# Attention output and expert activations placed 96 instead of 64 bytes behind a 128-byte boundary of SBUF

## The chip, the core and the metric

The kernel runs on one core of a Trainium2 chip. The metric is the device time of one execution in microseconds (us). The engines are named as in the profile: PE is TensorE's matmuls, PEld its weight loads (the load of the operand that stays in the array), DVE is VectorE, ACT is ScalarE, POOL is GpSimd, SP is SyncE, which issues most transfers.

## What is computed

A gated block of a Flamingo-like model, in float32, on 32 sequences of 128 tokens of width 256:

```python
x = x + tanh(g_xattn) * xattn(layernorm(x), ctx)          # 16 heads of 64, inner width 1024
x = x + tanh(g_ffn)   * moe(layernorm(x))

# xattn: q = x @ Wq, k = ctx @ Wk, v = ctx @ Wv; softmax(q k^T / 8) v; then  out @ Wo + bo
# moe:   logits = x @ gate_w.T ; two of eight experts for each token, at most 1024 tokens an expert
#        h  = relu(de @ fc1_w.T + fc1_b)      (256 -> 1024)
#        eo = h @ fc2_w + fc2_b               (1024 -> 256)
#        out = sum over the two experts of eo * gate
```

## The kernel before, in words

The program has two stages, one after the other.

**Attention** (`attention`) goes through 8 groups of 4 sequences (512 tokens), and in each through 8 pairs of heads: 64 steps. The products are split: each operand is cut into a high part of type float32r and a low part, the rest, also float32r, and a product is three matmuls (high by high, high by low, low by high). ACT writes the high part out of PSUM (line 698), DVE subtracts and writes the low part (line 809). The output of the heads is kept that way in `aT_h` and `aT_l`, 8 x 512 columns each. Once in a group PE multiplies them with the output weights: `project_out`, lines 558 to 560, in two bursts of 48 matmuls, one into `query_bank`, one into `out_bank`. There `aT_h` or `aT_l` is the stationary operand (128 columns, so 512 bytes of each partition) and `wo_h` or `wo_l` the moving one (256 columns). The last group is done in pieces at the end (lines 654 to 656).

**Experts** (`experts`) goes through 16 halves of experts, 512 token slots each. For each half PE runs, in this order: 48 matmuls *up* of 512 columns (lines 1195 to 1197; stationary `w1_h`/`w1_l`, moving `rT_h`/`rT_l`), 8 transposes of the next half's rows (line 1179; stationary `rows`, moving `ident`), and 96 matmuls *down* of 256 columns (lines 1209 to 1211; stationary `hid_h` and `hid_l`, moving `w2_h`/`w2_l`, which for every second expert are the tiles called `w_split` in the profile). After each sixth *up* matmul ACT writes `hid` (line 1245), DVE casts it to `hid_h` (line 1304) and subtracts for `hid_l` (line 1306). Of each *down* tile DVE adds the bias into `eo_raw` (line 1315), ACT scales it (line 1253) and POOL scatters it (line 1151). The rows of an expert come from the DRAM tensor `disp` by one transfer a half, in pieces of 1032 bytes, to `rows_0` or `rows_1`; POOL's indirect transfers out of `packed` filled `disp` in the attention stage (line 407).

The order of the work is written out by hand on every engine, with semaphores between them. Tiles are allocated in the order of the calls, one behind the other, each from a multiple of 32 bytes. Three tiles that nobody reads or writes shift what lies behind them. `round_up` (1824 bytes) puts the weights at byte 20480 of each partition. `line_up` stands in front of `aT_h`, `line_up_hid` in front of `hid_h`:

```python
ROUND_UP = (20480 - 18656) // 4
LINE_UP = 64 // 4
...
    pT = sb("pT", [P, 2, TOK])
    sb("line_up", [P, LINE_UP])
    aT_h, aT_l = sb("aT_h", [P, NP, TOK], f32r), sb("aT_l", [P, NP, TOK], f32r)
    packed = sb("packed", [P, GB, W])
...
    hid = [sb(f"hid{n}", [P, TOK]) for n in range(2)]
    sb("line_up_hid", [P, LINE_UP])
    hid_h, hid_l = sb("hid_h", [P, HK, TOK], f32r), sb("hid_l", [P, HK, TOK], f32r)
    eo_raw = sb("eo_raw", [P, GB, D])
    rows = [sb("rows_0", [P, GB, W])]
```

In the built program the tiles begin at these bytes of a partition (remainder by 128):

| tiles | before | remainder |
|---|---|---|
| w1, w2, wq, wk, wv, wo parts; xT, c parts; q_sb, k_sb, v_sb, work, probs_odd, pT; rT_h, rT_l, hid | many | 0 |
| ident | 17888 | 96 |
| aT_h, aT_l, packed | 182336, 198720, 215104 | 64 |
| tri, ones, iota, bias_o, gate_sb | 219232 and on | 96 |
| logitsT | 222432 | 96 |
| hid_h, hid_l, eo_raw, rows_0, rows_1 | 122944, 139328, 155712, 159808, 164032 | 64 |
| b2_0, b2_1 | 168160, 169184 | 96 |

Of the kernel before, what the change touches and what calls it, by code (L numbers as in the profile page):

```python
# [25 lines left out]
BIG = 65536.0  # L26
V_AHEAD = 2
ROUND_UP = (20480 - 18656) // 4
LINE_UP = 64 // 4


def pass_gate(eng, sem):
# [87 lines left out]
def attention(nc, ctx, block, sem, x_v, out_v, disp, ctxT, g_x, g_f, wq, wk, wv, wo, bo, gateT, fc1T, fc2, shared):  # L120
# [4 lines left out]
    def sb(name, shape, dt=f32):  # L125
        return ctx.enter_context(nc.sbuf_tensor(name, shape, dt))
# [23 lines left out]
# [3 lines that stand above are left out]
# [895 lines left out]
def experts(nc, ctx, block, sem, out_rows, disp, fc1T, fc1b, fc2, fc2b, shared):  # L1048
# [4 lines left out]
    def sb(name, shape, dt=f32):  # L1053
        return ctx.enter_context(nc.sbuf_tensor(name, shape, dt))
# [7 lines left out]
# [3 lines that stand above are left out]
# [290 lines left out]
```

## Time and profile before

| | |
|---|---|
| runs of the kernel | 995.57 us median of 3 (991.43, 995.57, 996.29) |
| the profiled execution | 994.87 us, its span 993.1 us |
| mean granted TensorE clock | 0.983 |
| busy: PE, PEld, DVE, ACT, POOL | 949.4, 823.4, 676.3, 508.1, 281.8 us |
| instructions | 18998 |

A page of the profile gives the busy time of each engine, the span in 40 slices, the transfers, the chain of waits that ended last, and the costliest groups of instructions. Matmuls are pipelined: each is shown with 0.28 us or so, from its start until its result is out, while the next one starts after some 0.12 us. So the distance between starts, or the length of a burst over the number of its matmuls, is what a matmul costs, and not its own duration.

### The profile page before, as it was taken

The numbers are of one execution on the slowest core, as the hardware profiler recorded it, in microseconds if no ns is written. First come the engines' busy times: TensorE is split into PE (matmuls) and PEld (weight loads), VectorE is DVE, ScalarE is ACT, GpSimd is POOL, SyncE is SP. The second block draws the span as 40 slices with busy tenths as digits, with TensorE's granted clock in tenths as the row PEclk, the third lists the DMA queues.
The fourth block names the chain that finished last, engine by engine and source line by source line (L and its number), as shares of the span: only waits on it lengthen the run. The fifth ranks groups of instructions, "written<-read, shape, count | busy, mean of one in ns | idle before, by whom it ended". The sixth has DMA issues, their size and how long they took to land.

```text
span 993.1 us, 18998 instructions
## 1 busy us (share of the span) xinstructions
PE 949.4 (96%) x7199; PEld 823.4 (83%) x7199; DVE 676.3 (68%) x1542; ACT 508.1 (51%) x1573; POOL 281.8 (28%) x293
## 2 busy tenths in 40 slices
PE   7799999999999999999999888999999999999996
PEld 5587877888878878878888786999999999999995
DVE  5768687686785886886776862757575665657572
ACT  3567376465664773673754621535444343435352
POOL 6803025024033043042041133222222223232222
PEclk8989999999999999999999998999999999999998
DMA  9096003011020021021011015254342435252521
GB/s 259 22 298 194 22 2 107 23 41 67 22 86 24 22 92 38 2 86 44 1 44 44 13 52 187 66 117 101 76 128 50 128 49 130 49 130 56 141 53 22
DMA packets 63099, 76.63 MB, mean 77 GB/s; under 512 B 6033, under 2 KB 55096, under 8 KB 63008
## 3 DMA queue, kind: packets, MB, share of 16 engines
q1 hardware_dynamic: 50720, 59.18, 20.0%
q0 software_dynamic: 12288, 16.23, 9.0%
q8 instruction: 58, 0.95, 0.4%
q14 instruction: 33, 0.27, 0.1%
HBM read 46.52 MB, written 29.49 MB: 77 GB/s over the span
## 4 chain that ended last, share of the span: by engine, by line
PE 73%; ACT 11%; DVE 8%; POOL 3%; DMA 2%; issue 2%; SPq 1%; POOLq 0%; DVEq 0%; another core or an unknown queue 0%
PE down L1211 6%; PE down L1210 6%; PE down L1209 6%; PE up L1195 6%; PE up L1196 6%; PE up L1197 6%; PE score L545 4%; ACT probs_odd L733 4%; ACT work L733 4%; PE out_bank L533 4%; PE probT L520 4%; DVE negmax L913 2%; PE rT L1179 2%; PE query_bank L466 2%; PE query_bank L464 2%
## 5 line engine op out<-in xcount | busy, mean ns | idle before, releaser
L1151 POOL DMA_INDIRECT out_dram<-eo,index x64 | 99.4, 1553 | 282.2 <-ACT eo L1253 250.4
L1245 ACT ACTIVATE hid<-up,b 128x512 f32<-128x512 f32 x128 | 88.3, 690 | 84.8 <-PE up L1197 84.8
L733 ACT ACTIVATE probs_odd<-score,negmax 128x128 f32<-128x128 f32 x256 | 91.3, 382 | 44.6 <-DVE negmax L913 44.6
L733 ACT ACTIVATE work<-score,negmax 128x128 f32<-128x128 f32 x256 | 91.4, 383 | 42.8 <-DVE negmax L913 42.8
L407 POOL DMA_INDIRECT disp<-packed,slots x64 | 68.8, 1075 | 133.8 <-DVE slots L904 92.4
L913 DVE TENSOR_REDUCE negmax<-score 128x4 f32<-128x512 f32 x128 | 82.0, 682 | 28.1 <-PE score L545 27.7
L698 ACT ACTIVATE k_sb<-key_bank 128x512 f32<-128x512 f32 x64 | 38.8, 606 | 112.8 <-PE key_bank L489 111.5
L1253 ACT ACTIVATE eo<-eo_raw,gate 128x256 f32<-128x256 f32 x64 | 30.9, 506 | 122.4 <-DVE eo_raw L1315 122.4
L1306 DVE TENSOR_TENSOR hid_l<-hid,hid_h 128x512 fp32r<-128x512 f32 x128 | 88.6, 693 | 4.4
L921 DVE COPY pT<-probT 128x512 f32<-128x512 f32 x128 | 82.2, 682 | 8.7 <-PE probT L520 7.4
L1315 DVE TENSOR_TENSOR eo_raw<-down,b 128x256 f32<-128x256 f32 x64 | 25.8, 423 | 86.4 <-PE down L1211 86.4
L545 PEld LDWEIGHTS score<-k_sb,q_sb 64*128 64x128 f32 x1024 | 66.8, 189 | 18.7 <-ACT q_sb L698 16.0
L545 PE MATMUL score<-k_sb,q_sb 64*128 64x128 f32 x1024 | 70.4, 277 | 11.7 <-ACT q_sb L698 11.7
L1304 DVE CAST hid_h<-hid 128x512 fp32r<-128x512 f32 x128 | 55.2, 432 | 33.1 <-ACT hid L1245 32.7
L1209 PE MATMUL down<-w_split,hid_h 128*128 128x256 f32 x256 | 72.6, 284 | 0.0
L533 PE MATMUL out_bank<-pT,v_sb 128*64 128x128 f32 x1008 | 69.8, 281 | 2.3 <-DVE xT_l L809 1.8
L1209 PE MATMUL down<-w_h,hid_h 128*128 128x256 f32 x256 | 72.0, 281 | 0.0
L1211 PE MATMUL down<-w_split,hid_l 128*128 128x256 f32 x256 | 71.9, 281 | 0.0
L1210 PE MATMUL down<-w_split,hid_h 128*128 128x256 f32 x256 | 71.9, 281 | 0.0
L1210 PE MATMUL down<-w_l,hid_h 128*128 128x256 f32 x256 | 71.3, 279 | 0.0
L1211 PE MATMUL down<-w_h,hid_l 128*128 128x256 f32 x256 | 71.3, 279 | 0.0
L533 PEld LDWEIGHTS out_bank<-pT,v_sb 128*64 128x64 f32 x1008 | 54.5, 138 | 10.6 <-DVE xT_l L809 3.1
(253 smaller groups left out, 2788.8 us busy)
## 6 DMA issues: line engine op xcount, KB each, us to landing
rows<-disp SPq DMA_DIRECT2D x18, 516.0 KB, 5.4
w_raw<-fc1T_dram SPq DMA_DIRECT2D x9, 1024.0 KB, 8.3
w_raw<-fc_dram SPq DMA_DIRECT2D x9, 1024.0 KB, 10.9
disp<-fixed SPq DMA_DIRECT2D x1, 8256.0 KB, 33.8
rows<-x_dram SPq DMA_DIRECT2D x16, 512.0 KB, 4.3
out_dram<-rows SPq DMA_DIRECT2D x8, 512.0 KB, 3.1
c_raw<-ctxT_dram SPq DMA_DIRECT2D x8, 256.0 KB
c_raw<-ctxT_dram SPq DMA_DIRECT2D x16, 128.0 KB
```

The costliest lines, as they stand in the source:

```text
L407: pool.indirect_dma_start(out=disp[:, :], out_offset=bass.IndirectOffsetOnAxis(ap=slots[:, j, b:b + 1], axis=0), in_=packed[:, b, :], in_o ...
L533: last = mm(bank[hh * DH:(hh + 1) * DH, b * P:(b + 1) * P], v_sb[:, j // 4, b, cols], pT[:, hh, b * P:(b + 1) * P], start=True, stop=True)
L545: last = mm(score[hh][:, t], q_sb[r, t], k_sb[u % 2][r, t], start=True, stop=True)
L733: last = nc.scalar.activation(probs[w % 2][:, c, :], score[hh][:, b * P:(b + 1) * P], ACT.Exp, bias=negmax[:, w % 2, c:c + 1], accum_out=s ...
L913: V.tensor_reduce(negmax[:, w % 2, hh * GB:(hh + 1) * GB], score[hh][:, :].rearrange("p (i k) -> p i k", i=GB), axis=AX, op=ALU.max, negat ...
L921: V.tensor_copy(pT[:, hh, :], probT[hh][:, :]).then_inc(pt_done, 1)
L1151: pool.indirect_dma_start(out=out_rows[:, :], out_offset=bass.IndirectOffsetOnAxis(ap=index[half][:, i:i + 1], axis=0), in_=eo[half][:, i, ...
L1209: mm(o, hid_h[:, k, t], w2_h[par][:, k, :], start=(k == 0), stop=False)
L1210: mm(o, hid_h[:, k, t], w2_l[par][:, k, :], start=False, stop=False)
L1211: last = mm(o, hid_l[:, k, t], w2_h[par][:, k, :], start=False, stop=(k == HK - 1))
L1245: nc.scalar.activation(hid[m % 2][:, :], up[m % 2][:, :], ACT.Relu, bias=b1[par][:, m:m + 1]).then_inc(s_hid, 1)
L1306: V.tensor_tensor(hid_l[:, m, :], hid[m % 2][:, :], hid_h[:, m, :].bitcast(f32), ALU.subtract).then_inc(s_hid_split, 1)
```

## The change

```diff
@@ -26,7 +26,7 @@
 BIG = 65536.0
 V_AHEAD = 2
 ROUND_UP = (20480 - 18656) // 4
-LINE_UP = 64 // 4
+LINE_UP = 96 // 4
```

Both `line_up` and `line_up_hid` grow from 64 to 96 bytes. Everything that is allocated behind them in its stage moves up by 32 bytes: in attention `aT_h`, `aT_l` and `packed` then begin 96 bytes behind a multiple of 128, `tri`, `ones`, `iota`, `bias_o`, `gate_sb` and `logitsT` on one, and the small statistics and routing tiles 32 bytes further; in the experts `hid_h`, `hid_l`, `eo_raw`, `rows_0` and `rows_1` begin 96 bytes behind, `b2_0` and `b2_1` on a multiple. `ident` and all weights stay. No instruction is added, taken away or moved on any engine or queue; only addresses in SBUF differ.

## Rows read from the trace of the kernel before

**Rows 1.** The page: busy time with share and count, and the slices of PE
```profile
PE 949.4 (96%) x7199; PEld 823.4 (83%) x7199; DVE 676.3 (68%) x1542; ACT 508.1 (51%) x1573; POOL 281.8 (28%) x293
...
PE   7799999999999999999999888999999999999996
```
**Rows 2.** Windows of both stages: stretch, length, busy by engine, clock, DMA share, GB/s
```profile
615.20:982.80 367.60, 367.60 (x2430) 336.43 (x2429) 235.48 (x447) 163.14 (x239) 95.68 (x62) 1.00 0.40 92
100.00:550.00 450.00, 441.10 (x3776) 370.87 (x3775) 336.27 (x846) 265.82 (x1054) 117.79 (x139) 1.00 0.13 42
```
**Rows 3.** Windows of the first three bursts of up, PE alone
```profile
615.20:626.20 11.00, 10.97 (x48) 0.99 0.56 203
638.42:649.34 10.92, 10.92 (x48) 1.00 0.95 235
684.21:695.12 10.91, 10.91 (x48) 1.00 0.95 226
```
**Rows 4.** Windows of bursts of down, PE alone: four of the sixteen
```profile
627.03:638.42 11.39, 11.39 (x96) 1.00 0.02 2
650.13:661.52 11.39, 11.39 (x96) 1.00 0.18 37
673.23:684.21 10.98, 10.98 (x96) 1.00 0.00 0
695.91:707.30 11.39, 11.39 (x96) 1.00 0.21 48
```
**Rows 5.** Windows of project_out into out_bank, PE alone: two of seven
```profile
106.32:111.97 5.65, 5.65 (x48) 1.00 0.01 3
...
384.87:390.31 5.44, 5.44 (x48) 1.00 0.02 3
```
**Rows 6.** Timeline of PE: start us, duration us, line, tiles; in the third burst
```profile
674.46 0.28 PE L1210 MATMUL down<-w_l,hid_h 128*128 128x256 f32 x1
674.58 0.28 PE L1211 MATMUL down<-w_h,hid_l 128*128 128x256 f32 x1
674.69 0.28 PE L1209 MATMUL down<-w_h,hid_h 128*128 128x256 f32 x1
```
**Rows 7.** Timeline of PE: bursts at full clock that are shorter than their loads
```profile
8.12 1.17 PE L112 MATMUL key_bank<-ident 128*128 128x128 f32 x9
```
**Rows 8.** The same, later
```profile
584.22 1.95 PE L685 MATMUL out_bank<-gate_sb,work 128*128 128x8 f32 x16
```
**Rows 9.** Instructions of single lines: duration ns min/median/max, first and last start
```profile
L1211 PEld LDWEIGHTS down<-w_split,hid_l x256: 187/188/188, 627.2 to 937.2; 128*128 128x128 f32 x128
...
L1306 DVE TENSOR_TENSOR hid_l<-hid,hid_h x128: 691/693/694, 618.2 to 972.4; 128x512 fp32r<-128x512 f32 x128
```
**Rows 10.** The same for ones as stationary operand
```profile
L591 PEld LDWEIGHTS query_bank<-mask,ones x14: 192/192/192, 140.6 to 557.8; 128*128 128x128 f32 x14
```
**Rows 11.** The same for line 698 and line 809 between 110 and 560 us
```profile
L698 ACT ACTIVATE aT_h<-out_bank x52: 597/609/614, 116.2 to 555.0; 128x512 fp32r<-128x512 f32 x52
...
L698 ACT ACTIVATE logitsT<-query_bank x7: 277/278/279, 127.2 to 544.3; 128x128 f32<-128x128 f32 x7
L698 ACT ACTIVATE xT_h<-query_bank x6: 597/599/600, 148.4 to 495.6; 128x512 fp32r<-128x512 f32 x6
```
**Rows 12.** The costliest groups: busy, mean ns of one, idle before and releaser
```profile
L1304 DVE CAST hid_h<-hid 128x512 fp32r<-128x512 f32 x128 | 55.2, 432 | 33.1 <-ACT hid L1245 32.7
```
**Rows 13.** Instructions of line 1315
```profile
L1315 DVE TENSOR_TENSOR eo_raw<-down,b x64: 410/425/427, 634.4 to 983.4; 128x256 f32<-128x256 f32 x64
```
**Rows 14.** The chain of waits between the stages: start us, us, what
```profile
604.54 2.40 DMA disp<-packed,slots
607.21 3.65 DMA rows<-disp
610.91 1.97 PE rT L1179 x8
```

## The prediction

> **What bounds the kernel.** I read the page first, then the windows by stage, the windows burst by burst, and last the starts of single matmuls. The page shows PE busy for 949.4 us of the 993.1, and in nearly every slice at nine tenths or more [rows 1]. By stage it is plainer: from 615.2 to 982.8 us, the experts, PE is busy for all of 367.6 us at full clock, DVE for 235.5, ACT for 163.1; from 100 to 550 us, attention, PE for 441.1 of 450 [rows 2]. So a microsecond of PE counts in full in the experts and nearly so in attention, and time on DVE, ACT or POOL counts only once its slack is gone.
>
> PE's time there is a number of matmuls by the distance between their starts. The chip shows two speeds for one and the same work. The reader should see this in the bursts of down: 96 matmuls take 11.39 us in one, and 10.98 us in the third [rows 4]. I read all sixteen: twelve take 11.39, and the four that take 10.98 are the first halves of the odd experts. The tiles and their addresses are the same in the second half of those experts, where a burst takes 11.39. Project_out does the same thing: 48 matmuls take 5.65 us in four of the seven bursts into out_bank, and 5.44 in the last three [rows 5]; the other seven follow the burst beside them, which makes eight slow and six fast. By matmul that is 5.65/48 = 118 ns against 5.44/48 = 113 ns, and inside a fast burst each start is 0.11 or 0.12 us behind the last [rows 6]. A burst keeps the speed with which it comes out of its first matmuls. A row for up shows nothing of it: 10.91 to 11.00 us for 48 matmuls of 512 columns, 227 ns each [rows 3]; up reads no tile that moves, except that it waits for DVE and ACT.
>
> **The change, part by part.** No instruction comes, goes or changes its place, so no count changes and no queue is passed by anything. What may change is the duration of instructions that touch a tile with a new address. Those are five kinds.
>
> *Loads of aT and hid as stationary operand*: 1536 in the experts' down, 672 in project_out, 48 in the last group. They lie under a matmul: a load takes 187 to 188 ns from start to end [rows 9], but one can start every 112 ns, as two bursts show whose matmuls are too short to hide it. Nine matmuls on ident, which lies 96 bytes behind a multiple of 128, take 1.17 us; less the last one's own 0.275 us, that is 0.90/8 = 112 ns [rows 7]. Sixteen with a stationary tile on a multiple of 128 take 1.95 us: (1.95 - 0.26)/15 = 113 ns, the first distance included [rows 8]. So a load from 96 costs what a load from 0 costs, and ones, at 96 too, is loaded in 192 ns [rows 10], like ident. I take no change in the interval of a load: 112 ns, below the 113 of a fast burst. The bounds: below, all bursts fast; above, all slow. Both ends are rows of the same work. All fast: 12 x (11.39 - 10.98) = 4.9 us and 8 x (5.65 - 5.44) = 1.7, so 6.6 us less. All slow: 4 x 0.41 = 1.6 and 6 x 0.21 = 1.3, so 2.9 us more. Since the speed already differs between bursts with the same addresses, I expect another mixture and no trend: 0 is my term.
>
> *Writes and reads of aT and hid by ACT and DVE*: ACT writes aT_h, at 64, in 609 ns and xT_h, at 0, in 599; logitsT, at 96, has a quarter of the columns and takes 278 [rows 11]. 599 - 278 = 321 ns for 384 columns is 0.84 ns a column, and 278 - 128 x 0.84 = 171 ns are fixed; nothing is left that would be due to an address. DVE needs 693 ns for hid_l [rows 9] and 432 for hid_h [rows 12]. Together 1.13 us for every six matmuls of up, which take 6 x 0.227 = 1.36 us. So even a loss there has 0.24 us, 21%, of cover in each of 128 blocks; this is what hides the term. 0.
>
> *Reads of b2 and writes of eo_raw*: b2 goes from 96 to 0, eo_raw from 64 to 96. The addition takes 425 ns [rows 13] and runs beside down, 4 in a burst of 11 us. Without that cover it would still be off PE's path. 0; the last one of the program alone stands on the path, with tens of nanoseconds at most.
>
> *Small tiles*: tri, ones, gate_sb and logitsT go from 96 to 0; they are loaded or read some 20 times in a group, at intervals that rows 7 and 8 show equal for 96 and 0. 0.
>
> *Transfers into rows and out of packed*: they run under PE's work, but for one: at the seam of the stages the last scatter of 2.40 us and the first load of rows of 3.65 us stand in the chain [rows 14]. The pieces of 1032 bytes start at a multiple of 8 bytes before and after; the load's nearest row is itself. I take 0, with 0.2 us either way. A rule of the Trainium skill speaks against the change here: "DMA: Bandwidth & Descriptors", section "How a descriptor splits into AXI transactions", says that a read transaction starts from a 256-byte boundary, and what lies between it and the start is fetched in beats of 32 bytes for nothing. If that held for the SBUF side of these pieces, each would need 36 beats instead of 35, an estimate from that page of 3% on the load, or 0.1 us more in the sum; no row of this trace shows two starts for one size, so it stays out.
>
> The sum: 994.87 us of the profiled execution plus 0 = 994.9. That execution is 0.7 below the median of the three runs, 995.57, and these runs spread over 4.9 us. That spread is the size of twelve bursts of down changing speed; whether that is its cause no row shows. I predict 995.0 us.
>
> **The rivals.** Less than half a per cent, or 5 us, either way is about what a measurement of this kernel can tell from no change, and I use that as the border.
>
> *All bursts fast.* The distance of a burst settles in its first three or four matmuls, by how load and matmul stand to each other. If 32 bytes more shift that for good, every burst takes 10.98 or 5.44 us: 994.9 - 6.6 = 988.3 us. For it: the two speeds exist, and PE has no slack. Against: the same addresses give both. To pass the border 10 of the 12 slow bursts and most of project_out must turn. 0.17.
>
> *All bursts slow.* 994.9 + 2.9 = 997.8 us, within the border. 0.10.
>
> *Slower: the load of a misplaced stationary tile becomes the bound.* 512 bytes that begin at 64 touch eight pieces of 64 bytes; at 96 they touch nine. If a load pays for pieces, its interval goes from 112 to 112 x 9/8 = 126 ns. It decides as soon as the interval is over 113 or 118 ns. Down would take 16 x 96 x 0.126 = 193.5 us instead of 12 x 11.39 + 4 x 10.98 = 180.6, so 12.9 more; project_out 672 x 0.126 = 84.7 instead of 8 x 5.65 + 6 x 5.44 = 77.8, so 6.9 more. 994.9 + 19.8 = 1014.7 us. For it: PEld is busy for 336 of the experts' 367.6 us [rows 2], so the load is only a few ns from being the bound. Against: ident's 112 ns at 96 [rows 7], where however the moving operand is short. 0.11.
>
> *Slower: DVE's writes of hid at 96 lose a quarter.* Its block would take 1.13 x 1.25 = 1.41 us and pass PE's 1.36, by 0.05 us in 128 blocks: 6 us, about 1001 us. Against: the addresses so far leave no mark on ACT and DVE [rows 11]. 0.04.
>
> **How the numbers follow.** The forecast, another mixture of fast and slow bursts, has 0.58. Faster by over 0.5% is the first rival, 0.17. Within 0.5%: 0.58 + 0.10 = 0.68. Slower: 0.11 + 0.04 = 0.15. The range begins at 988.0, under the all-fast case, and ends at 1000.0: the all-slow 997.8, with the spread of the runs, 0.7 to 1.4 us from the profiled one, and the transfer's 0.2. What it leaves out is the slower side, 0.15.
>
> **What would show it.** The windows of the sixteen bursts of down and the fourteen of project_out should again read 11.39 or 10.98 and 5.65 or 5.44, in other places perhaps; up should stay at 10.9. LDWEIGHTS of hid should stay at 188 ns, hid_l at 693, aT_h at 609, the cast at 432. A burst of down over 11.4 us, or loads with a new duration, would make the load rival right; idle time of PE behind hid_split would point to DVE. If all bursts read 10.98, the address sets the speed, and my reading that it is chance is wrong.

## The result, and the profile after

| | before | after |
|---|---|---|
| median of 12 runs (lowest, highest), us | 995.17 (991.43, 998.09) | 1000.39 (997.41, 1002.15) |
| profiled execution's span, us | 993.1 | 998.5 |
| ratio after/before, 95% interval | | 1.0049 (1.0035 to 1.0064) |

The change costs 4.9 us (3.5 to 6.4). The forecast was no change, with 988 to 1000 us as its range; the median lies 0.4 above its end, and the interval leaves no room for no change.

The page of the profile after, busy time of each engine; it answers to [rows 1]:

```profile
PE 954.1 (96%) x7199; PEld 828.0 (83%) x7199; DVE 675.9 (68%) x1542; ACT 508.7 (51%) x1573; POOL 281.4 (28%) x293
```

The same instructions; PE is busy for 4.7 us more (949.4 before) and PEld for 4.6 (823.4 before), DVE, ACT and POOL for less than 1 us more or less. So the loss is in PE's own work, not in a wait. The windows of the bursts of down, PE alone (stretch, length, busy, clock, DMA share, GB/s), against [rows 4]; the first four of the sixteen:

```profile
629.73:641.07 11.34, 11.34 (x96) 1.00 0.01 1
652.78:664.26 11.48, 11.48 (x96) 1.00 0.19 35
675.96:687.44 11.48, 11.48 (x96) 1.00 0.01 1
699.14:710.62 11.48, 11.48 (x96) 1.00 0.19 40
```

All further ones read 11.48. Neither 11.39 nor 10.98 is there any more. Project_out into out_bank, against [rows 5]:

```profile
106.41:112.04 5.63, 5.63 (x48) 1.00 0.01 3
176.64:182.33 5.69, 5.69 (x48) 1.00 0.00 0
246.68:252.31 5.63, 5.63 (x48) 1.00 0.00 0
```

5.63 and 5.69 in place of 5.65 and 5.44. Up, which reads no tile that moved, is as it was but for its first burst, which starts at the low clock (0.95 on the average of its window, 1.00 in the second):

```profile
617.50:628.93 11.43, 11.43 (x48) 0.95 0.55 197
641.07:651.99 10.92, 10.92 (x48) 1.00 0.97 238
```

By starts of matmuls in the trace, the mean step from one to the next within a burst was 117.8 or 113.3 ns before and is 118.7 or 117.3 ns now. This leaves out the first steps: the first of a burst of down takes 0.20 us, so the length over 96 is up to 1.1 ns more (11.39/96 = 118.6, at a step of 117.8). The steps have also become uneven. Behind the first few of a burst they went from 117 to 119 ns in a slow one before and were 113 or 114 in a fast one; in the second burst after, they go from 116 to 122. Its timeline (start us, duration us, line, tiles), where [rows 6] had 0.12 and 0.11:

```profile
653.46 0.28 PE L1211 MATMUL down<-w_split,hid_l 128*128 128x256 f32 x1
653.58 0.28 PE L1209 MATMUL down<-w_split,hid_h 128*128 128x256 f32 x1
...
654.05 0.28 PE L1210 MATMUL down<-w_split,hid_h 128*128 128x256 f32 x1
654.18 0.28 PE L1211 MATMUL down<-w_split,hid_l 128*128 128x256 f32 x1
654.30 0.28 PE L1209 MATMUL down<-w_split,hid_h 128*128 128x256 f32 x1
654.41 0.28 PE L1210 MATMUL down<-w_split,hid_h 128*128 128x256 f32 x1
```

The rest of what the prediction named stayed where it was. Single lines after (duration ns min/median/max), against [rows 9, 13]:

```profile
L1211 PEld LDWEIGHTS down<-w_split,hid_l x256: 187/188/193, 629.9 to 942.2; 128*128 128x128 f32 x128
...
L1306 DVE TENSOR_TENSOR hid_l<-hid,hid_h x128: 691/693/694, 620.9 to 977.9; 128x512 fp32r<-128x512 f32 x128
```

```profile
L1315 DVE TENSOR_TENSOR eo_raw<-down,b x64: 414/425/426, 637.0 to 989.0; 128x256 f32<-128x256 f32 x64
```

The seam in the chain of waits after, against [rows 14]:

```profile
606.78 2.42 DMA disp<-packed,slots
...
609.47 3.66 DMA rows<-disp
```

**Where the 4.9 us are.** Down: 11.34 + 15 x 11.48 = 183.5 us against 12 x 11.39 + 4 x 10.98 = 180.6, so 2.9 more. Project_out, by the speeds of its fourteen bursts: six at 117.3 ns and eight at 118.7, 6 x 5.63 + 8 x 5.70 = 79.38 us against 8 x 5.65 + 6 x 5.44 = 77.84, so 1.5 more. Together 4.4. The first burst of up adds 0.4 in this trace (11.43 against 11.00), by its clock; whether it belongs to the change isn't shown.

### The profile page after: what moved, and what is told of

It reads as the page before. It is cut to its first block, busy times and chain, and to the rows that moved or that the text cites. A ratio compares the mean times of both kernels' runs of the same rounds, so it can differ in the third digit from the quotient of the medians.

```text
span 998.5 us, 18998 instructions
## 1 busy us (share of the span) xinstructions
PE 954.1 (96%) x7199; PEld 828.0 (83%) x7199; DVE 675.9 (68%) x1542; ACT 508.7 (51%) x1573; POOL 281.4 (28%) x293
## 4 chain that ended last, share of the span: by engine, by line
PE 71%; ACT 12%; DVE 9%; POOL 3%; DMA 2%; issue 2%; SPq 1%; another core or an unknown queue 0%; POOLq 0%; DVEq 0%
PE down L1211 6%; PE down L1210 6%; PE down L1209 6%; PE up L1195 6%; PE up L1196 6%; PE up L1197 6%; ACT work L733 4%; ACT probs_odd L733 4%; PE score L545 4%; PE out_bank L533 3%; PE probT L520 3%; DVE negmax L913 2%; PE rT L1179 2%; PE query_bank L558 1%; ACT aT_h L698 1%
```

## The theories

- **Place**: a stationary tile that begins at 96 is dearer to load or read than one at 64, wherever the other operand is.
- **Distance**: what counts is how far the stationary operand's start lies behind the moving operand's, beyond a whole multiple of a larger step. That was 64 bytes and is now 96. Each distance has speeds of its own. (The larger step is written as 128 here. In every run the starts within a burst differ by a multiple of 512 bytes plus 0, 32, 64 or 96, since the slices of aT and hid are 512 bytes apart and those of the weights 1024. So no run tells 128 from 256 or 512.)
- **Start (chance)**: the way a burst starts picks its speed and the address only shifts that.
- **Other tiles**: not hid or aT, but rows, eo_raw or packed, which moved with them.

The expectations call place and distance together the load theory (or, each for itself, the absolute and the relative theory).

## Experiments: which tiles

All runs below are compared with the kernel before on the same chip. Three chips were used, and the kernel's median differs between them: it was 995.4 us beside the first four, 990.2 beside the next four and 992.5 beside the last four, so ratios are compared, not times. Each row of the windows shown is one burst of down, PE alone.

**experts96**: the pad of the experts alone.

```diff
-    sb("line_up_hid", [P, LINE_UP])
+    sb("line_up_hid", [P, 96 // 4])
```

> Only the tiles of the experts from hid_h on begin at 96; attention stays at 64. Load theory (how a weight load of hid meets the running matmul depends on where hid begins): fifteen or sixteen bursts of down at 11.48 us, none at 10.98, project_out still 5.65 or 5.44, about 3 us (0.3%) slower than before. Chance theory (the start of a burst decides, the address doesn't): some bursts at 10.98 again, time within 0.1% of before.

Measured: 1.0026 (1.0009 to 1.0044).

```profile
625.83:637.31 11.48, 11.48 (x96) 1.00 0.03 3
649.01:660.49 11.48, 11.48 (x96) 1.00 0.19 39
```

All sixteen at 11.48: 16 x 11.48 - 180.6 = 3.1 us more, against 2.6 measured (0.9 to 4.4). Project_out reads 5.54 or 5.33 us from its first start to its last, the speeds of 117.8 and 113.3 ns, as before. The load theory holds for down; chance doesn't.

**attention96**: the pad of attention alone.

```diff
-    sb("line_up", [P, LINE_UP])
+    sb("line_up", [P, 96 // 4])
```

> Only the tiles of attention from aT_h on begin at 96; the experts stay at 64. Load theory: project_out in a pattern of its own, no burst at 5.44; the down bursts at 11.39 and 10.98 as before; 1 to 2 us (0.1 to 0.2%) slower than before. If the loss is mainly in attention, by waits rather than by the bursts: 3 us or more slower. Chance theory: project_out at 5.65 and 5.44 again.

Measured: 1.0017 (0.9999 to 1.0035).

```profile
655.52:666.91 11.39, 11.39 (x96) 1.00 0.22 47
678.62:689.60 10.98, 10.98 (x96) 1.00 0.00 0
```

Down is as before, with the same four fast bursts. Project_out: eight bursts at 117.3 and six at 118.7 ns, so 8 x 5.63 + 6 x 5.70 = 79.2, 1.4 us more, against 1.7 measured, with an interval that just touches none. The two halves add up within their intervals: 2.6 + 1.7 = 4.3 us, against 4.9.

**hid96**: hid at 96, eo_raw and rows back to 64 by another pad. (A fourth unused tile, `line_up_rows` of 96 bytes between rows_0 and rows_1, is the same in all the kernels here.)

```diff
-    sb("line_up_hid", [P, LINE_UP])
+    sb("line_up_hid", [P, 96 // 4])
     hid_h, hid_l = sb("hid_h", [P, HK, TOK], f32r), sb("hid_l", [P, HK, TOK], f32r)
+    sb("line_up_eo", [P, 96 // 4])
     eo_raw = sb("eo_raw", [P, GB, D])
```

> Experts: hid_h and hid_l begin at 96, but a further pad of 96 bytes puts eo_raw and both tiles of rows back to 64; attention stays at 64. Load theory: the same bursts as with all experts' tiles moved, 11.48 us each, about 3 us slower than before. If the rows, eo_raw or their transfers carry it (another tile theory): bursts of down at 11.39 and 10.98 as before, and no loss.

Measured: 1.0009 (0.9993 to 1.0025), so 0.9 us more (0.7 less to 2.5 more), under the 3 us that were expected. By the total this run doesn't decide. By the bursts it does:

```profile
675.93:687.41 11.48, 11.48 (x96) 1.00 0.01 1
699.12:710.47 11.35, 11.35 (x96) 1.00 0.19 42
```

Twelve of 11.48 and four of 11.35 (117.3 ns, the second speed that project_out showed after the change), none at 11.39 or 10.98. From the first matmul of up to the last of down this trace has 370.3 us, against 367.9 before. So hid alone carries the loss in down; rows, eo_raw and their transfers don't. Only which bursts get 11.35 changed with them. Why the total rose by less than these 2.4 us isn't known.

## Experiments: place or distance

**all32**: the weights and all behind them up by 32 bytes. hid and aT begin at 96 as in the change, their moving operands at 32.

```diff
-ROUND_UP = (20480 - 18656) // 4
+ROUND_UP = (20480 + 32 - 18656) // 4
 LINE_UP = 64 // 4
```

> LINE_UP stays 64, but everything from the weights on moves up by 32 bytes: hid and aT begin at 96 and the moving operands, which began on a multiple of 128, at 32. Absolute theory (where the stationary tile begins counts): bursts of down at 11.48 us as in the changed kernel, 1000 us. Relative theory (the distance of 64 between stationary and moving operand counts): bursts at 11.39 and 10.98, about 995 us. Up, whose operands both move, stays at 10.91 in either.

Measured: 0.9997 (0.9980 to 1.0014).

```profile
629.14:640.54 11.40, 11.39 (x96) 1.00 0.02 2
652.24:663.23 10.99, 10.99 (x96) 1.00 0.21 48
674.94:685.91 10.97, 10.97 (x96) 1.00 0.00 0
697.61:709.01 11.40, 11.40 (x96) 1.00 0.20 44
```

Eight of sixteen at the fast speed, eight at the slow, 113.3 and 117.8 ns. With hid at the very address of the changed kernel the loss is gone. That ends the theory that the stationary tile's place decides. The moving tile's place alone doesn't either: it is 0 in the kernels before and after and in both apart runs below, with four sets of speeds. What the shift did change is which bursts are fast, and how many: eight here, four before, at the same distance.

**moving32**: the same shift with LINE_UP at 32. hid and aT keep 64, the moving operands begin at 32.

```diff
-ROUND_UP = (20480 - 18656) // 4
-LINE_UP = 64 // 4
+ROUND_UP = (20480 + 32 - 18656) // 4
+LINE_UP = 32 // 4
```

> The weights and everything behind them begin at 32, aT and hid stay at 64 themselves, so that the distance is 32. Distance theory: 118.3 ns and 11.43 to 11.45 us a burst, as with apart32, where hid was at 32 and the moving operand at 0; 0.2 to 0.4% slower than before. Place theory (what counts is where hid begins): 117.8 and 113.3 ns.

Measured: 1.0061 (1.0046 to 1.0075).

```profile
627.40:638.84 11.44, 11.44 (x96) 1.00 0.02 3
650.55:662.00 11.45, 11.45 (x96) 1.00 0.19 39
```

118.3 ns in every burst of down and project_out: the speed that the distance theory named from apart32, below. Place would have left 117.8 and 113.3. The total misses what was expected: 6.1 us more (4.6 to 7.4, from four executions), while the bursts give about 4. By the trace, the experts account for 2.3 (370.2 us from the first matmul of up to the last of down, against 367.9), and project_out for 1.6. The other 2 us or so lie ahead of the experts, since behind down the trace has 9.9 us, against 10.0. What they are isn't known.

**apart0** and **apart32**: hid and aT at 0 and at 32, the moving operands at 0, what lies behind hid and aT held at 64.

```diff
-    sb("line_up", [P, LINE_UP])
     aT_h, aT_l = sb("aT_h", [P, NP, TOK], f32r), sb("aT_l", [P, NP, TOK], f32r)
+    sb("line_up_pk", [P, 64 // 4])
...
-    sb("line_up_hid", [P, LINE_UP])
     hid_h, hid_l = sb("hid_h", [P, HK, TOK], f32r), sb("hid_l", [P, HK, TOK], f32r)
+    sb("line_up_eo", [P, 64 // 4])
```

(These lines are apart0's. apart32 keeps the two pads in front, at 32 bytes, and its two new ones are of 32.)

> aT and hid begin on a multiple of 128, as their moving operands do (distance 0); packed, eo_raw and rows stay at 64 as before. The all32 run showed that the distance counts, not the place. If the speed follows the distance, every burst has one of a few speeds that belong to distance 0, none of them a mixture of 117.8 and 113.3 ns, nor of 118.7 and 117.3. If only distances of 64 differ from all others (64 is the half of a 128-byte piece), it reads like 96: 11.48 us a burst of down, about 1000 us.

> aT and hid begin 32 bytes behind, distance 32 from the moving operands; packed, eo_raw and rows stay at 64. If distances 32 and 96 are alike (both a quarter of 128 away from 0): 118.7 and 117.3 ns, 11.48 us a burst, about 3 us slower in the experts than before. If each distance has speeds of its own: others than those four.

Measured: apart0 1.0071 (1.0053 to 1.0089), apart32 1.0033 (1.0021 to 1.0045). A window of each, first apart0:

```profile
648.77:660.37 11.60, 11.60 (x96) 1.00 0.19 33
```

```profile
647.04:658.48 11.44, 11.44 (x96) 1.00 0.18 37
```

At distance 0 every burst runs at 120.0 ns, the slowest of all, and its loads are longer too (hid_l's in apart0, against 188 before):

```profile
L1213 PEld LDWEIGHTS down<-w_split,hid_l x256: 188/192/192, 625.7 to 939.8; 128*128 128x128 f32 x128
```

At distance 32 every burst runs at 118.3 ns, neither 96's speeds nor a mixture. So the guesses that all distances but 64 are alike, and that 32 is like 96, both fall. The totals, 7.0 and 3.3 us more, go with the bursts: 16 x 11.60 - 180.6 = 5.0 us in down for apart0, and 16 x 11.44 - 180.6 = 2.4 for apart32, with project_out beside.

| distance | runs | ns from matmul to matmul | burst of down, us |
|---|---|---|---|
| 0 | apart0 | 120.0 | 11.60 |
| 32 | apart32, moving32 | 118.3 | 11.44 |
| 64 | before, attention96 (down), all32, lowfirst, kick64, kickpart, kickboth | 117.8 or 113.3 | 11.39 or 10.98 |
| 96 | after, experts96, hid96, kick96 | 118.7 or 117.3 | 11.48 or 11.35 |

Two limits. Up, with matmuls of 512 columns, has both operands at the same offset in every run (distance 0), at 227 ns, so nothing here says whether it depends on the distance. The transposes of rows, with matmuls of 128 columns, went from rows at 64 and ident at 96 to both at 96 with the change: 109 ns from one to the next both times.

## Experiments: what picks one of the two speeds

**kick64** and **kick96**: one more matmul of 64 columns in front of each burst of down, at distance 64 and 96. Its result goes to a half of down's bank that nobody reads.

```diff
+            pe.wait_ge(s_hid_split, 8 * n + 1)
+            if not (isinstance(n, int) and n == 0):
+                pe.wait_ge(s_eo_raw, 4 * n - 3)
+            mm(down[0][:, D:D + 64], w1_h[par][:, 0, 0:P], w1_h[par][:, 0, 0:64], start=True, stop=True)
             for k, i in [(k, i) for tiles in ((0, 1), (2,), (3,)) for k in range(HK) for i in tiles]:
```

> As before (distance 64) with one more matmul of 64 columns in front of each burst of down, into an unused part of down's bank. Start theory (at distance 64 the way a burst starts picks one of two speeds, which it then keeps): the set of fast bursts changes, all 10.98 plus at most 0.1 us for the added matmul at best (about 4 us faster), or all 11.39; never another speed than 117.8 or 113.3 ns. If something else that differs between the groups sets the speed (what ACT, DVE or a transfer does meanwhile): the third burst and every fourth after it stay the fast ones.

> The changed kernel (distance 96) with the same added matmul in front of each burst of down. Start theory: bursts choose between 118.7 and 117.3 ns, and no start reaches 113.3 ns, since that speed isn't there at distance 96; within 0.2% of the changed kernel. If the distance only shifted the start: bursts of 10.98 us appear, 4 us or more faster than the changed kernel.

Measured: kick64 0.9988 (0.9977 to 0.9998), kick96 1.0048 (1.0032 to 1.0064). The windows of kick64 (97 matmuls, since the added one still overlaps):

```profile
622.70:633.68 10.98, 10.98 (x97) 1.00 0.01 1
645.50:656.48 10.98, 10.98 (x97) 1.00 0.15 28
668.29:679.68 11.39, 11.39 (x97) 1.00 0.01 1
691.50:702.47 10.97, 10.97 (x97) 1.00 0.20 45
```

and of kick96:

```profile
621.24:632.58 11.34, 11.34 (x97) 1.00 0.03 3
644.40:655.87 11.47, 11.47 (x97) 1.00 0.13 19
```

In kick64 the set is turned round: the twelve bursts of 11.39 us take 10.98, and the four of 10.98 take 11.39. No instruction of ACT, DVE or a queue was edited, so what changed with the added matmul is how a burst starts, and that picks the speed. It picks among those of its distance: at 96 the same added matmul changes nothing in down, and 113.3 ns isn't reached. The total gained little: eight fewer slow bursts give 3.3 us, sixteen added matmuls of 0.1 take 1.6, and 1.2 (0.2 to 2.3) were measured.

What sets the start without an added matmul isn't shown. Two pairs of runs with hid at one distance differ in the set: before and all32 (four and eight fast), experts96 and hid96 (none and four at 11.35). In both pairs rows, the stationary tile of the eight transposes just ahead of each burst, begins at 64 in one and at 96 in the other, with ident at 96. That they set it is a guess; no run moves rows alone.

**lowfirst**: the three products of down in another order.

```diff
-                mm(o, hid_h[:, k, t], w2_h[par][:, k, :], start=(k == 0), stop=False)
-                mm(o, hid_h[:, k, t], w2_l[par][:, k, :], start=False, stop=False)
-                last = mm(o, hid_l[:, k, t], w2_h[par][:, k, :], start=False, stop=(k == HK - 1))
+                mm(o, hid_l[:, k, t], w2_h[par][:, k, :], start=(k == 0), stop=False)
+                mm(o, hid_h[:, k, t], w2_h[par][:, k, :], start=False, stop=False)
+                last = mm(o, hid_h[:, k, t], w2_l[par][:, k, :], start=False, stop=(k == HK - 1))
```

> As before (distance 64), with the three products of a step of down in another order: low part of hid first, then the high part twice. The same loads and matmuls. Start theory: the set of fast bursts changes or not, but the speeds are 117.8 and 113.3 ns again, since all loads of hid stand at the same distance. If the order of stationary tiles (the same one twice in a row) makes the slow speed: other speeds than these two.

Measured: 1.0005 (0.9993 to 1.0017), and the same four bursts are fast, at the same two speeds. This other order of the tiles makes no difference.

**kickpart**: the added matmul only where it helps.

```diff
-            mm(down[0][:, D:D + 64], w1_h[par][:, 0, 0:P], w1_h[par][:, 0, 0:64], start=True, stop=True)
+            if not (e % 2 == 1 and half == 0):
+                mm(down[0][:, D:D + 64], w1_h[par][:, 0, 0:P], w1_h[par][:, 0, 0:64], start=True, stop=True)
```

> As kick64, but without the added matmul in the first half of each odd expert, whose burst of down was fast before and slow with it. Start theory: all sixteen bursts of down at 10.98 us; PE's time in the experts about 364 us (367.9 before, less 4.9, plus twelve added matmuls of 0.1), time 0.3 to 0.5% under before. If the groups influence each other (a burst's state comes from the burst before it): other bursts turn slow, and the gain is that of kick64, 0.1%.

Measured: 0.9970 (0.9959 to 0.9981), faster than the kernel before and than the changed one.

```profile
624.52:635.49 10.97, 10.97 (x97) 1.00 0.01 1
647.31:658.29 10.98, 10.98 (x97) 1.00 0.14 27
670.00:680.98 10.98, 10.98 (x96) 1.00 0.00 0
692.79:703.76 10.97, 10.97 (x97) 1.00 0.18 37
```

All sixteen at 10.98. From the first matmul of up to the last of down the trace has 364.1 us, against 367.9 before: 4.9 less for the bursts, 1.2 more for twelve added matmuls of 0.1. The time fell by 3.0 us (1.9 to 4.1).

**kickboth**: kickpart, and one matmul in front of each first burst of project_out.

```diff
+            if b0 == 0:
+                mm(bank[:, 0:64], wo_h[:, 0, 0:P], wo_h[:, 0, 0:64], start=True, stop=True)
             for i in range(2):
```

> As kickpart, and one matmul of 64 columns in front of each first burst of project_out as well. Start theory: the start of a burst decides there too, so the speeds of project_out change against before, to 113.3 ns at best (up to 3 us less where all fourteen were slow), never anything but 117.8 and 113.3. In all 0.3 to 0.7% under before. If waits set the start there, the speeds stay mixed as before and the time is kickpart's.

Measured: 0.9994 (0.9981 to 1.0008). A miss. Eight bursts of project_out ran at 113.3 ns and six at 117.8, a mixture as without it (kickpart, with project_out untouched, has eight and six too, in other groups). One more matmul doesn't set the speed there. That the start hangs on waits that differ between groups and executions is likely, but not shown. The 2.4 us against kickpart aren't in the experts, which take 364.4 and 364.1 us; in the two traces the first transpose of the experts comes 1.6 us later. Why isn't known.

Project_out is where chance does play. At the same addresses, distance 64, its fast bursts number six of fourteen in the trace before, eight in experts96, hid96, lowfirst and kickpart, and none in kick64; between none and eight lie 1.7 us. At distance 96 all fourteen ran at 117.3 ns in kick96, 0.3 us less in all than the fourteen of kick64 at 117.8. So the 1.5 us of project_out hold for the two traces compared and can be less, or none, in others.

## Why the prediction was wrong, point by point

- **What bounds the kernel**: right. PE's distance from matmul to matmul was what the change touched, and each of its microseconds counted.
- **"The bounds: below, all bursts fast; above, all slow", and the forecast of another mixture: this step failed.** It took 11.39 and 10.98 us for the only two speeds there are. They are those of distance 64. Distance 96 has 11.48 and 11.35, so the bound above, 1.6 + 1.3 = 2.9 us more, was too low, and the likeliest case, a mixture of the same two speeds with a mean near zero, didn't exist: all four fast bursts of down were lost (2.0 us) along with the six of project_out. The predicted 0 measured 2.9 + 1.5 = 4.4 us in the bursts.
- **"All bursts slow", 997.8 us, given 0.10**: nearest to what came, and right in its direction, but with the old slow speed. That the total missed the range by 0.4 us only is luck: the range's end had been put 2.2 us above this rival for the spread of the runs.
- **"A load from 96 costs what a load from 0 costs"**: right in itself, and misleading. [Rows 7 and 8] measure loads beside matmuls that are too short to matter. The loss lies in how a load and a matmul of 256 columns run side by side, and for that no row at another distance was read. This should have widened the range on both sides.
- **The load rival, 126 ns from nine pieces instead of eight**: wrong too, though it had the right sign. Loads took 187 to 194 ns after the change, and hid at 96 did no harm in all32.
- **DVE and ACT, b2 and eo_raw, small tiles**: 0, as said: 693, 608 and 425 ns again (608 where 609 was).
- **The count of 48 loads in the last group**: it is 96 (768 matmuls read aT, 672 of them in project_out). No term of the sum used it.
- **Transfers**: 0. The load at the seam took 3.65 us before and 3.66 after, all 18 loads 5.4 in the median both times. By the estimate from the Trainium skill's page "DMA: Bandwidth & Descriptors", section "How a descriptor splits into AXI transactions", 3% more, it would have taken 3.76; these rows show no such cost on the SBUF side.
- **"These runs spread over 4.9 us. That spread is the size of twelve bursts"**: not by down. Its pattern is the same in three executions with the experts' tiles where they were and no added matmul (before, attention96, lowfirst). The first transpose of the experts comes at 610.2, 616.2, 613.9 and 612.4 us in the first four experiments, 6 us apart, while the experts behind it take 366.9 to 370.8; so most of the spread arises ahead of the experts. The changing bursts of project_out can be 1.7 us of it; the rest wasn't traced.
- **"The address sets the speed, and my reading that it is chance is wrong"**: the last sentence of the prediction named what turned out, though only with all bursts fast as its sign.

The Trainium skill, in "TensorE: Matmul & The Clock Gate", section "Step-by-step: what each phase is for", says that loading the next tile's weights doesn't take read bandwidth from the running matmul, since each has its own port. The measurement differs: with the same instructions, operands 0 bytes apart give 120.0 ns and operands 64 apart 117.8 or 113.3, and moving both by 32 bytes leaves the speeds as they were. So the pace depends on the two addresses together, which speaks for the two reads getting in each other's way. That they do is inferred from the addresses alone, and through what, no run shows.

## What to carry to other kernels

Where PE is the bound and a weight load nearly fills a matmul's time, look at the distances between starts of matmuls, not at their durations: more than one value for the same work means that something other than the work sets it. Try a few distances (0, 32, 64 and 96 bytes beyond a multiple of 512 were tried here) between where the stationary and the moving tile begin; keep both in mind whenever a tile in front of them changes its size. If two speeds remain, a small matmul in front of a burst can select the better one, but only where the burst starts the same way each time.

## What was not expected of the hardware

- Matmuls of 256 columns with a fresh load of 128 columns each, both operands float32r at full clock: 120.0, 118.3, 117.8 or 113.3, and 118.7 or 117.3 ns at distances of 0, 32, 64 and 96 bytes. Moving both operands by 32 bytes left the two speeds of distance 64 as they were, though other bursts had them.
- At distance 64 a burst keeps one of two speeds for 96 matmuls, 4% apart, and one matmul of 64 columns ahead of it switched them in all sixteen bursts of down, but set nothing in project_out.
- Still open: what the two reads share; why hid96 has four bursts at 117.3 ns and the changed kernel one, and all32 eight at 113.3 and the kernel before four; some 2 us of moving32; distances that aren't multiples of 32, and those of 128 to 480 bytes, which weren't tried.
